# Attention step reordered; the transposed keys leave PSUM through VectorE instead of ScalarE

## The reference

```python
h = tok(x, mask, ...)                         # embeddings summed, LayerNorm       (16 x 128 tokens, width 256)
h = h + attn(layernorm(h), Wk, Wq, Wv, Wo, bo, ...)
h = h + ffn(layernorm(h), gate_w, expert_bias, w1, w2, w3)

def attn(x):                                  # 16 heads of width 16, causal
    k, q, v = (x @ W for W in (Wk, Wq, Wv))   # split into heads
    k, q = layernorm(k) * kw + kb, layernorm(q) * qw + qb       # per head, over 16 numbers
    p = softmax(where(causal, q @ k.T / 4, -inf))
    return (p @ v) @ Wo + bo

def ffn(x):                                   # 8 experts, the best 2 of each token, hidden width 704
    s = softmax(x @ gate_w.T); sel = top2(s + bias)
    return sum over the 2 of  (silu(x_e @ w1[e]) * (x_e @ w3[e])) @ w2[e],  x_e = x * s[e]
```

## Time and profile before

| | |
|---|---|
| median of 3 runs | 560.64 us (559.51 to 562.48) |
| the profiled execution | 562.17 us |
| its span, first to last instruction | 560.0 us |
| TensorE busy | 509.3 us, 91% of the span |
| ScalarE, VectorE, GpSimd busy | 258.1, 286.1, 270.3 us |
| mean granted TensorE clock | 0.958 |
| attention, first to last scores | 29.9 to 201.6 us |

### The profile page before, as it was taken

How to read it: one execution, slowest core, us unless ns; L and a number is a source line. 1 busy time by engine, 2 the same in 40 slices (tenths; PEclk the granted TensorE clock), 3 DMA queues, 4 the chain that set the end, 5 groups by cost and what they waited for, 6 DMA issues and landing times.

```text
span 560.0 us, 12788 instructions
## 1 busy us (share of the span) xinstructions
PE 509.3 (91%) x4212; PEld 431.8 (77%) x4213; DVE 286.1 (51%) x710; ACT 258.1 (46%) x591; POOL 270.3 (48%) x503
## 2 busy tenths in 40 slices
PE   6788999999999886289999999999999999999991
PEld 2345767776777674169999999999999999999981
DVE  3686888788887656933333333333333333333330
ACT  1068899989988872043223332233322333322320
POOL 4587786777663201142444444443444444444432
PEclk9899999999999986589999999999999999999996
DMA  4017611000137673001211222112221122222221
GB/s 161 9 51 270 205 39 57 28 28 28 56 123 226 198 228 121 20 29 30 32 28 37 38 38 36 24 35 38 38 38 28 29 38 38 38 29 29 37 38 20
DMA packets 29480, 36.62 MB, mean 65 GB/s; under 512 B 7792, under 2 KB 23024, under 8 KB 29456
## 3 DMA queue, kind: packets, MB, share of 16 engines
q0 software_dynamic: 8352, 12.76, 13.3%
q1 hardware_dynamic: 20288, 22.51, 12.3%
q10 hardware_dynamic: 816, 1.06, 0.5%
HBM read 26.81 MB, written 9.50 MB: 65 GB/s over the span
## 4 chain that ended last, share of the span: by engine, by line
PE 81%; DVE 6%; POOL 3%; issue 3%; DMA 3%; ACT 3%; ACTq 0%; POOLq 0%; DVEq 0%
PE PS L1276 34%; PE PS L1287 18%; PE PS L1060 10%; PE PS L1146 7%; PE PS L1227 3%; PE PS L1107 3%; PE PS L1122 2%; PE PS L1099 2%; DMA x_pair<-word_dram,idx 1%; ACT work L566 1%; PE PS L1159 1%; DMA out_dram<-x_pair,dst_c 1%; DVE front L785 1%; DMA work<-x_rows,src_c 1%; POOL rstd L398 1%
## 5 line engine op out<-in xcount | busy, mean ns | idle before, releaser
L1276 PEld LDWEIGHTS PS<-work,arena 128*128 128x128 f32 x1716 | 197.6, 192 | 3.8 <-ACT work L670 2.0
L1276 PE MATMUL PS<-work,arena 128*128 128x128 f32 x1716 | 198.1, 276 | 1.5 <-ACT work L670 1.5
L676 ACT ACTIVATE work<-PS 128x768 f32<-128x768 f32 x39 | 31.6, 810 | 197.2 <-PE PS L1276 197.2
L1287 PE MATMUL PS<-w_sb,work 128*128 x468 | 107.6, 380 | 0.7 <-DVE x_pair L1035 0.7
L1027 DVE TENSOR_TENSOR work<-work,PS 128x640 f32<-128x640 f32 x39 | 32.0, 822 | 139.5 <-ACT work L676 139.5
L1287 PEld LDWEIGHTS PS<-w_sb,work 128*128 128x128 f32 x468 | 86.1, 191 | 11.0 <-issue 1.1
L513 POOL DMA_INDIRECT out_dram<-x_pair,dst_c x39 | 79.9, 2048 | 22.0 <-POOL dst_c L512 20.5
L566 ACT ACTIVATE work<-PS,nmax 128x128 f32<-128x128 f32 x256 | 72.5, 403 | 4.5 <-DVE nmax L795 4.5
L512 POOL COPY dst_c<-dest_i 128x1 int32 (+1 forms) x39 | 7.1, 182 | 137.2 <-DVE x_pair L1035 134.9
L666 ACT ACTIVATE arena<-w_sb 128x1408 f32 x40 | 55.1, 1377 | 17.8 <-DVE er_i L1000 12.8
L1060 PE MATMUL PS<-ident,work 128*128 128x128 f32 x336 | 56.5, 283 | 2.8 <-ACT work L566 2.6
(11 more groups left out here) (147 smaller groups left out, 610.4 us busy)
## 6 DMA issues: line engine op xcount, KB each, us to landing
w_sb<-w_dram SPq DMA_DIRECT2D x16, 640.0 KB, 6.2
w_sb<-w_dram SPq DMA_DIRECT2D x8, 704.0 KB, 4.7
x_rows<-x SPq DMA_DIRECT2D x16, 128.0 KB, 1.9
out_dram<-arena SPq DMA_DIRECT2D x16, 128.0 KB, 2.1
w_sb<-w_dram SPq DMA_DIRECT2D x16, 64.0 KB, 6.3
w_sb<-w_qkv_dram ACTq DMA_DIRECT2D x1, 768.0 KB, 7.9
work<-x_rows,src_c POOLq DMA_INDIRECT x41, 2.8
out_dram<-x_pair,dst_c POOLq DMA_INDIRECT x39, 4.2
```

The source lines that it names most:

```text
L1276: last = n.matmul(up_ps[p][:, i, c, :], ws[p][:, k, at:at + P], xT_sb[p][:, k, :], start=(k == 0), stop=(k == DK - 1))
L1287: last = n.matmul(PS[:, 7, 0:D], hT_sb[p][:, i, :], w2_sb[:, bass.ds(e, 1), i, :], start=(i == 0), stop=(i == FK - 1))
```

## The change

The diff does six things:

- VectorE gets `keys_out(u)`: behind its four maxima it copies the transposed keys out of `T_BANK`, with scale and bias, and raises the new semaphore `k_ready`. ScalarE waits for `k_ready` and copies only the queries.
- TensorE projects queries and keys of t+2 before the outputs of t-1 and not after them.
- The aT transposes go to the upper half of `VY_BANK`; `var_f` is now waited for by the outputs in every step, the wait for `aT_ready` moves from the outputs to the values, and the aT transposes wait for `v_ready`.
- `outputs_back` moves behind `keys_to_rows(1)` and `x2_to_rows`; the second mask matmul moves behind the Wo product.
- ScalarE takes `squares` and the queries before `outputs_out`, and `normalized_out` before `transposed(1)`. VectorE takes `squared_sums` before the reciprocal.
- The last four transposes of the exponentials are each let go by their own exponential (`exp_group`) and not all by the last.

```diff
+        k_ready = sem("k_ready"); exp_group = sem("exp_group")
@@ ScalarE
                         last = a.activation(probs[...], PS[:, r, g * P:(g + 1) * P], ACT.Exp, bias=...)
+                        if r == RG - 1 and g < GROUPS - 1:
+                            last.then_inc(exp_group, 1)
                 def queries_and_keys_out(u):
-                    act.wait_ge(qk_ps, u + 1)
+                    act.wait_ge(k_ready, u + 1)
-                    for dst, at, c in ((qT[0], 0, 0), (qT[1], 0, 2), (kT, D, 4)):
+                    for dst, at, c in ((qT[0], 0, 0), (qT[1], 0, 2)):
-                    a.activation(aT[p]..., PS[:, O_BANK, 0:D],
+                    a.activation(aT[p]..., PS[:, VY_BANK, D:2 * D],
                 if valid(t):
                     exponentials(0)
                     exponentials(1)
+                if valid(t + 2):
+                    squares(t + 2)
+                if valid(t + 1):
+                    queries_and_keys_out(t + 1)
                 if valid(t - 1):
                     outputs_out(t - 1)
-                if valid(t + 1):
-                    queries_and_keys_out(t + 1)
-                if valid(t + 2):
-                    squares(t + 2)
...
                     exponentials(2)
-                    transposed(1)
                 if valid(t - 1):
                     normalized_out(t - 1)
                 if valid(t):
+                    transposed(1)
                     exponentials(3)
@@ VectorE
+                def keys_out(u):
+                    dve.wait_ge(qk_ps, u + 1)
+                    if not isinstance(u, int) or u > 0:
+                        dve.wait_ge(s_done, RG * u)
+                    v.tensor_scalar(kT..., PS[:, T_BANK, D:2 * D], cols_sb[:, 4:5],
+                                    cols_sb[:, 5:6], ALU.mult, ALU.add).then_inc(k_ready, 1)
...
                     squared_sums(1)                       # step -1
+                    keys_out(0)
...
                     maxima(3)
                 if at_step(t, 0):
                     normalize_qk(1)
+                if valid(t) and valid(t + 1):
+                    keys_out(t + 1)
...
+                if valid(t + 2) and valid(t):
+                    squared_sums(t + 2)
                 u = t - 1                                 # reciprocal and product of the outputs
...
-                if valid(t + 2) and valid(t):
-                    squared_sums(t + 2)
@@ TensorE
                 def outputs(u):
-                    wait(pe, aT_ready, u + 4)
-                    if edge and t + 2 >= B:
-                        wait(pe, var_f, u)
+                    wait(pe, var_f, u)
...
                 def keys_to_rows(r):
-                    pe.wait_ge(exp_done, RG * t + r + 1)
-                    if r == RG - 1:
+                    if r < RG - 1:
+                        pe.wait_ge(exp_done, RG * t + r + 1)
+                        transposes(probs[...], GROUPS, r).then_inc(probsT_ps, 1)
+                    else:
                         wait(pe, logits_read, t - 1)
                         wait(pe, qk_ready, t + 2)
-                    transposes(probs[...], GROUPS, T_BANK if r == RG - 1 else r).then_inc(probsT_ps, 1)
+                        for g in range(GROUPS):
+                            if g < GROUPS - 1:
+                                pe.wait_ge(exp_group, (GROUPS - 1) * t + g + 1)
+                            else:
+                                pe.wait_ge(exp_done, RG * t + r + 1)
+                            last = transposes(probs[... one group], 1, T_BANK, g * P)
+                        last.then_inc(probsT_ps, 1)
                 def values(u):
-                    pe.wait_ge(aT_ready, u + 1)
+                    wait(pe, aT_ready, u + 2)             # u + 1 for the first
...
                     pe.wait_ge(a_ready, u + 1)
-                    wait(pe, var_f, u - 3)
                     wait(pe, aT_ready, u)
-                    transposes(a_n, DK, O_BANK).then_inc(aT_ps, 1)
+                    wait(pe, v_ready, u - 1)
+                    transposes(a_n, DK, VY_BANK, D).then_inc(aT_ps, 1)
...
-                    outputs(t - 1)                        # was ahead of project(t + 2)
                     project(u, aT[p], QK_BANK, 0, 2 * D, qk_done)
+                    outputs(t - 1)
                     keys_to_rows(0)
-                    outputs_back(t - 1)
                     keys_to_rows(1)
                     x2_to_rows(t - 2)
+                    outputs_back(t - 1)
                     values(t + 1)
...
                     keys_to_rows(2)
-                    mask_bank(t + 1, 1)
                     (Wo product)
+                    mask_bank(t + 1, 1)
```

More of the change, by code:

```diff
@@ L202, in build_tower @@
             sem("aT_ps"), sem("aT_ready"), sem("qk_done"), sem("v_done"), sem("v_ready"), sem("sq_ready"))
-        qkn_ready, qk_ps, qk_ready = sem("qkn_ready"), sem("qk_ps"), sem("qk_ready")
-        s_done, max_done, exp_done = sem("s_done"), sem("max_done"), sem("exp_done")
+        qkn_ready, qk_ps, qk_ready, k_ready = sem("qkn_ready"), sem("qk_ps"), sem("qk_ready"), sem("k_ready")
+        s_done, max_done, exp_done, exp_group = sem("s_done"), sem("max_done"), sem("exp_done"), sem("exp_group")
         probsT_ps, probsT_ready, pv_done, o_ready = (
@@ L615, in step @@
                     wait(act, v_done, u - 1)
-                    a.activation(aT[p].rearrange("p k s -> p (k s)"), PS[:, O_BANK, 0:D],
+                    a.activation(aT[p].rearrange("p k s -> p (k s)"), PS[:, VY_BANK, D:2 * D],
                                  ACT.Copy).then_inc(aT_ready, 1)
@@ L844, in first_norm @@
                     link(v.scalar_tensor_tensor(row(u), tmp, rstd[:, 0:1], beta, ALU.mult, ALU.add))
+                def keys_out(u):
+                    dve.wait_ge(qk_ps, u + 1)
+                    if not isinstance(u, int) or u > 0:
+                        dve.wait_ge(s_done, RG * u)
+                    v.tensor_scalar(kT.rearrange("p b s -> p (b s)"), PS[:, T_BANK, D:2 * D], cols_sb[:, 4:5],
+                                    cols_sb[:, 5:6], ALU.mult, ALU.add).then_inc(k_ready, 1)
                 if at_step(t, -4):
@@ L880, in step @@
                     normalize_qk(1)
+                if valid(t) and valid(t + 1):
+                    keys_out(t + 1)
+                if at_step(t, 0):
                     first_norm(3)
@@ L1135, in keys_to_rows @@
                 def keys_to_rows(r):
-                    pe.wait_ge(exp_done, RG * t + r + 1)
-                    if r == RG - 1:
+                    if r < RG - 1:
+                        pe.wait_ge(exp_done, RG * t + r + 1)
+                        transposes(probs[:, r * 512:(r + 1) * 512], GROUPS, r).then_inc(probsT_ps, 1)
+                    else:
                         wait(pe, logits_read, t - 1)
                         wait(pe, qk_ready, t + 2)
-                    transposes(probs[:, r * 512:(r + 1) * 512], GROUPS,
-                               T_BANK if r == RG - 1 else r).then_inc(probsT_ps, 1)
+                        for g in range(GROUPS):
[3 more added lines that the diff above has]
+                                pe.wait_ge(exp_done, RG * t + r + 1)
+                            last = transposes(probs[:, r * 512 + g * P:r * 512 + (g + 1) * P], 1, T_BANK, g * P)
+                        last.then_inc(probsT_ps, 1)
                 def project(u, a, bank, w0, w, done):
@@ L1163, in values @@
                 def values(u):
-                    pe.wait_ge(aT_ready, u + 1)
+                    if isinstance(u, int) and u == 0:
+                        pe.wait_ge(aT_ready, 1)
+                    else:
+                        wait(pe, aT_ready, u + 2)
                     wait(pe, v_ready, u)
@@ L1192, in step @@
                     transposes(qkn, 2 * DK, T_BANK).then_inc(qk_ps, 1)
-                if valid(t - 1):
-                    outputs(t - 1)
                 u = t + 2
@@ L1199, in step @@
                     project(u, aT[p], QK_BANK, 0, 2 * D, qk_done)
+                if valid(t - 1):
+                    outputs(t - 1)
                 if valid(t):
                     keys_to_rows(0)
-                if valid(t - 1):
-                    outputs_back(t - 1)
                 if valid(t):
@@ L1219, in step @@
                     keys_to_rows(2)
-                if valid(t + 1) and valid(t):
-                    mask_bank(t + 1, 1)
                 u = t - 1
@@ L1229, in step @@
                     last.then_inc(wo_done, 1)
+                if valid(t + 1) and valid(t):
+                    mask_bank(t + 1, 1)
                 if at_step(t, B - 2):
```

## The result

| | before | after |
|---|---|---|
| median (20 runs each, same chip) | 560.47 us (558.03 to 562.48) | 562.80 us (560.20 to 564.84) |
| profiled execution, its span | 562.17, 560.0 us | 562.89, 561.0 us |

The ratio is 1.0039, with a 95% interval of 1.0027 to 1.0050: about 2.2 us more, where I had forecast 0.75 less. That is inside the range and within the 0.5%, but the sign is wrong, and the difference is clear of the noise. It is not a matter of the mean clock: the mean granted clock of the 20 runs of the changed kernel is 0.965, and in the four groups of 23 to 29 runs of the kernel before that were taken beside the experiments it is 0.964 to 0.965.

The account below looks back on a forecast made before the run. TensorE was taken as the bound in attention, busy 10.82 of 11.08 us a step. Middle -0.2, first steps +0.2 and last steps -0.75 gave about -0.75 from 560.64: 559.9 us, range 556.0 to 563.5.

Parts of the forecast that it names:

- First steps: Step 0: keys_out ahead of GpSimd's statistics makes GpSimd 0.5 later, step 1 wins 0.3 back; +0.2 us, bounds -0.2 and +0.7.
- sign of being wrong: The prediction is wrong if the middle period moves by more than 0.25, or an edge by more than 2 us.
- The middle: Middle steps: a period of 11.11 against the mean of 11.13, -0.02 a step, -0.2 us in twelve.
- B: Rival: VectorE is not late at outputs_to_rows; period 10.87, -0.26 a step, 556.9 us with the edges; chance 0.25.
- The load of the projection: Behind aT's copy on TensorE: load starts 0.05 behind the copy, at 102.67; 102.87 taken as a bound.
- C: Rival: the projection's first load is as late as the outputs' was, +0.2; period 11.22, 561.2 us; chance 0.15.
- The product's end: VectorE's product of the outputs done at 108.23 in the step starting at 100.73, delaying outputs_to_rows; 0.24 us charged a step.
- ScalarE's wait for aT: In a middle step, ScalarE's wait for aT becomes longer by 0.3 to 0.45, from 1.31 before.
- GpSimd's chain: squared_sums comes 1.0 earlier, so GpSimd's chain does too; nothing waits for it in a middle step.
- The last steps: Steps 14 and 15 without the keys and with transposes ahead of a wait: -0.75 us; bounds 0 and 2 together.
- the 0.35: Step 14, where TensorE waited for the copies of queries and keys to transpose x2: 0.35 us saved.
- the 0.4 of step 15: Step 15, where TensorE waited for outputs_out with keys_to_rows(1) and x2 queued behind it: 0.4 us saved.

Follow-up runs that it names:

- e1: Changed kernel, but in step -1 VectorE copies the keys of sequence 0 before normalization and squared sums; 561.48 against 561.22 us for the kernel before, ratio 1.0010.
- e6: Changed kernel, but ScalarE copies the keys of sequence 0 as before the change; 561.99 against 560.64 us for the kernel before, ratio 1.0022.
- e8: e6, with ScalarE copying queries and keys of sequence 0 ahead of the squares of sequence 1; 562.32 against 560.50 us for the kernel before, ratio 1.0028.
- e11: e8, with the keys of sequence 1 also copied by ScalarE; 560.60 against 560.52 us for the kernel before, ratio 0.9992.
- e5: Changed kernel with its new orders, but ScalarE copies all keys again; 566.03 against 560.64 us for the kernel before, ratio 1.0100.
- e2: e1, with VectorE's squared sums moved back behind the product of the outputs; 568.21 us, ratio 1.0133 to the kernel before.
- e9: e8, with VectorE's centering of sequence t+4 moved behind the product; 561.36 against 560.50 us for the kernel before, ratio 1.0009.
- e12: e11, with VectorE's centering of sequence t+4 moved behind the product; 559.86 against 560.52 us for the kernel before, ratio 0.9988.
- e10: e4, with the outputs' back transposes behind bank 1's and x2's from step 14 on; 560.60 against 560.50 us for the kernel before, ratio 0.9995.
- e4: Kernel before, with only the last four exponential transposes each waiting for their own exponential; 560.27 against 561.22 us for the kernel before, ratio 0.9987.
- e3: Kernel before, with only the keys copied by VectorE behind its maxima (first in step -1); 561.48 against 561.22 us for the kernel before, ratio 1.0007.
- b2: The kernel before, unedited, run once more for a second trace; 560.72 us, span 558.6.
- e7: e6, with VectorE's centering of sequence t+4 moved behind the product; 561.47 against 560.64 us for the kernel before, ratio 1.0014.
- a2: The changed kernel, unedited, run once more for a second trace; 563.90 us, span 561.8.

## Why the prediction was wrong

**The step that failed** is "First steps". It costed one thing, `keys_out(1)` ahead of GpSimd's statistics in step 0 (GpSimd 0.5 late, 0.3 won back in step 1: +0.2, bounds -0.2 to +0.7). Measured are +3.0 and +3.4, and so the prediction's own sign of being wrong, an edge that moves by more than 2 us, came true.

Its two terms were mis-sized. In e1, e6 and e8 GpSimd starts on these statistics 12.64 behind the first `normalize_qk`, before 11.74: 0.90 late, not 0.5, and e11, which takes `keys_out(1)` away, has `normalize_qk` of sequence 2 back in its place. And step 1 wins nothing back: from that `normalize_qk` to the scores of step 2 it takes 10.61 in e1 and 10.55 in e6 where before has 10.21, and `outputs_back` waits for `outputs_out` there (0.74 in e1). Together they are the 1.2 to 1.3 of e1 and e6.

The larger part was put at nothing because it was not looked at: in step -1 both engines' new orders put the first queries and keys behind work that waits for the projection of sequence 1. The rows stood in the trace of before (ScalarE at 28.25 and 29.97), and the diff shows both edits. The first scores come 3.4 late, and GpSimd's statistics at 14.84, 2.20 later than in e1. e5 shows that 2.1 of such lateness leaves `normalize_qk` of sequence 2 in its place; the rest, and the clock that falls behind the stall, does not.

How much of the 2.20 is the order and how much the clock no run separates, since the clock fell in both traces of the changed kernel. An estimate from its rows: TensorE has no pause from the scores (33.32) over the filler to the transposes of queries and keys (39.37), so a filler of 3.19 and not 4.88 would have brought them 1.69 earlier. By that up to 1.7 is the clock's, and at least 0.5 the order's.

**The middle: right, by its own steps.** Predicted 11.11 a step against 11.13; measured -0.45 over the eleven periods of steps 2 to 12, -0.04 a step, and with step 13 nothing. The sum started from a step of 11.08 and set its 11.11 against the mean of 11.13, so the sign of its -0.02 was no finding. Step by step the gain is uneven: steps 4 to 9 take 66.84 against 66.86, which is nothing; steps 10 to 12 take 10.98, 10.91 and 10.89 against 11.08 each; step 2 gains 0.21 and step 3 loses 0.24. So well inside the loop the new order wins nothing, and only steps 11 and 12, where `outputs_to_rows` loads 7.58 and 7.55 behind the scores and not 7.65, come near B's period. The load of the projection 0.05 behind the copy was right, so C is refuted. `keys_out` takes 0.54, not 0.42, and moves what is behind it by 0.45, the upper bound, not 0.34. The product's end (+0.10) and the values' end both came later than summed, and met as the sum had them; B did not happen. From the load of `outputs_to_rows` to the next scores it took 3.39 where the sum had 3.56, and that made up for it; that two misses cancel is luck, and the 11.11 is better than its terms. ScalarE's wait for aT did not grow (1.29, before 1.31), as I had said it would: what it gained it waits for oT. GpSimd's chain was called free, and e2 shows the move of `squared_sums` to be a condition of the whole order.

**Step 13 was left out.** The selection of the first batch of tokens runs on VectorE at the end of step 12 and `normalize_qk` comes behind it, 1.36 behind the scores (182.44), before 0.65 (179.12). The timeline of weight loads:

```profile
183.16 0.42 PEld L1074 LDWEIGHTS PS<-ident,arena 128*128 128x128 f32 x4 [0.78 <-DVE arena L819]
```

The step takes 11.56 to 11.58 in the traces of after, e1, e6 to e9, e11 and e12, 11.11 before. That the new order leaves VectorE no room to make up the selection is a reading; nothing was tried there.

**The last steps: right in sign, by luck.** Predicted -0.75, measured -2.3 and -1.0, for another reason. The windows of the 7 us from about 4.4 behind the last scores, before and after:

```profile
205.00:212.00 7.00, 6.63 (x30) 5.55 (x31) 3.41 (x10) 4.44 (x14) 0.00 (x0) 0.54 0.87 263
```

```profile
208.00:215.00 7.00, 3.84 (x33) 3.19 (x31) 4.75 (x12) 5.02 (x15) 0.00 (x0) 1.00 0.88 276
```

Both traces of before have the clock at 0.54 here, both of after at 1.00. Some 30 matmuls and transposes keep TensorE busy for 6.63 or 3.84 us. I had priced only the waits of the earlier trace rows. Of these, step 14 gave 0.11 (10.99 against 11.10) for the 0.35, and the 0.4 of step 15 is nothing, as e10 against e4 shows. From the scores of step 15 to `er_i` it is 38.0 in both traces of before, 36.7 in e3 (only the keys moved) and 36.7 in e4 (only `exp_group`), both at 1.00 there, and 35.9 and 37.2 in the two of after. That the edits kept the clock up is not shown: it is two traces of before against one of each.

**Two rules beside the rows.** The Trainium skill (VectorE: DVE Perf Modes, section "The DRAIN you can't avoid") has the next operation wait for the pipe to empty. The row behind `keys_out` (107.78) starts 0.09 before its end (107.87). The same section adds that an operation that is not held starts earlier, which the prediction left out; so the trace does not contradict it, and the 0.08 a step that the prediction read from it was not there. The Trainium skill (ScalarE: Activation LUTs, section "Rules for kernel authors") has multiply and add on VectorE up to 3 times faster in bf16; here, in f32 out of PSUM, the same copy takes 0.54 on VectorE and about 0.5 on ScalarE (two in 1.01), and the 2 us that the prediction worked out from the factor did not come. Neither rule moved the time.

## What to carry to other kernels

In a software pipeline written out by hand, a new order has to be walked through the first and last steps as well as the middle: an instruction that finds its input ready in every middle step may be the one that stands in front of the only work there is in the first. When two edits each look like nothing, price them together: here, in the mean of steps 4 to 12, the keys' move is worth 0.02 a step alone, the new order costs 0.29 alone, and together they win 0.05. And before counting on an engine being early, add up what lies between its last input and its result: 0.81 us under a cover of 0.5 is late, however early the engine is ready.

## What the hardware showed that I had not expected

- TensorE's granted clock is down to 0.50 for some 3 to 4 us of steps -1 to 1 in 8 of the 16 traces, and not in every one with the same idle time of TensorE ahead of it: behind 3.34 us in both traces of the changed kernel; behind 2.43 in e8, e10, e11 and e12, and not in before, b2, e4 or e9; behind 2.16 in e3; behind 2.05 in e7, and not in e5 or e6. What decides it is open. What it costs depends on the slack behind it: e10 and e4 are the same up to step 13, and with the fall the scores of step 1 come 1.36 later (18.28 against 16.92) and those of step 2 at 29.22 against 29.18.
- A start repaired by 2.1 us (e8 against e6, scores of step 0 at 3.06 and 5.18) gave nothing: S2 30.57 and 30.46, ratios 1.0028 and 1.0022. What ended last was GpSimd's chain, not the scores.
- In the last steps the clock is at 0.54 over 7 us in both traces of before, and in the 14 others it is at 1.00 for at least the first 6 of these 7 us. The time from the scores of step 15 to `er_i` goes with it: 38.0 in those two; 37.2 where the clock goes down 10.5 to 11.5 us behind these scores and stays down (a2, e5, e11); 36.7 to 36.9 where it goes down at 12.4 to 13.4 (e1, e3, e4, e6 to e10, e12); 35.9 in after, where it is down from 11.4 to 15.4 but up again to 18.4, and in e2, where it goes down at 17.2.
